# Gated cross-attention with a binarised feed-forward product on one core: rows of the large product split before they are turned, and turned by DMA

## Chip, core and metric

One core of one Trainium2 chip. The metric is the device time of one execution in microseconds (us). The engines are TensorE (PE), VectorE (DVE), ScalarE (ACT), GpSimd (POOL) and SyncE (SP), the last here only a queue that issues DMAs.

## What is computed

```python
def _L0_xattn_ref(query, key):
    a = jnp.einsum('bqd,bkd->bqk', query, key)
    e = jax.nn.softmax(a, axis=-1)
    return jnp.einsum('bqk,bkd->bqd', e, key)

def _L0_ffn_ref(x, weight_real, bias):
    W = mean(|weight_real|, per row) * sign(weight_real)
    return jnp.einsum('bsi,oi->bso', x, W) + bias

x = x + jnp.tanh(g_xattn[0]) * _L0_xattn_ref(_layernorm(x), ctx_4096)
x = x + jnp.tanh(g_ffn[0]) * _L0_ffn_ref(_layernorm(x), weight_real, bias)
```

x is (4, 1024, 2048) f32, the keys are (4, 64, 2048), the weight is 2048 x 2048.

## The kernel before

The 4096 rows of x are 32 tiles of 128 rows. A tile t goes through three stages. Stage one: its row statistics (`norm_stats1`, L678, from the row buffer `xr`), the factors of the first normalisation (`rstd1` on GpSimd, `place_factors`, and on TensorE `spread_factors`, L1067), normalisation of a second copy of the rows that lies in quadrants (`xs1`, `normalise1`, L518), the turn of rows into columns by VectorE (`turn_q`, L701), and the split into a high and a low f16 part `qt` (`high_q` on ACT, L533, `low_q` on VectorE, L721). Stage two, attention: `scores` (L1074), the maximum (`max_logits`, L732 on), `exp` (L545), `split_probs` (L742 to L748), `transpose_probs` on TensorE (L1080), `copy_pt`, and in four chunks of 512 columns `attend` (L1088) and `add_attention` (L754), each with its row statistics (`norm_stats2`); then `rstd2`, `normalise2` into `xn2` (L526), and on GpSimd `add_bias` (L455). Stage three, the large product: the normalised rows must be turned so that the 2048 columns lie on partitions. Before the change SyncE moves `xn2` into quadrants `xs2` by four DMAs (`move_x1`, L296), VectorE turns it back into `xn2` in two instructions (`turn_x1`, L701), and then `high_x1` (ACT, L541) and `low_x1` (VectorE, L726) split it into `x1t`, which has two slots. TensorE computes chunk n of y with the signs of the weights (`ffn_block`, L1096) in four blocks of 8 matmuls; VectorE scales it (`scale_y`, L765) and adds it to the rows (`add_y`, L773); SyncE stores the rows (`store`, L376).

Every engine runs a list in a fixed order, and semaphores tie the lists together. The steady part is `step(t)`: TensorE runs the 16 blocks of tile t (k = 0 to 15, n = k // 4) and, between blocks, the attention of tile t + 2 and the spread of tile t + 3. The constants in lines 75 to 79 say behind which block each piece stands: before, scores behind block 2, the transpose of the probabilities behind 4, the four `attend` behind 6 to 9, the spread behind 8. The scores wait for `q_set`, the first block of chunk n waits until the bank that it writes is free, which is `y_scaled` of two chunks before: block 8 waits for `scale_y(t, 0)`, block 0 for `scale_y(t-1, 2)` (L1165).

VectorE's order in a step (L966 to L1001) is: `finish_y(t-1, 3)`, `turn_x1(t+1)`, `max_logits` and `split_probs` of t+2, `low_x1(t+1)`, four `norm_stats1` of tile t+3, `scale_y(t, 0)`, `norm_mean1`, `add_y(t, 0)`, the four `add_attention` with their statistics and `place_factors`, `finish_y(t, 1)`, `turn_q(t+3)`, `finish_y(t, 2)`, `low_q(t+3)`. ACT's order (L651 to L664) is `high_x1(t+1)`, `exp`, `copy_pt`, `normalise1(t+3)`, `normalise2(t+2)`, `high_q(t+3)`. SyncE's order (L398 to L411) is `store(t-1)`, the reload of the same row buffer with tile t+3 once the store has landed (L380), `load_quadrants(t+3)` (L310), at one step in four the next batch's keys, and `move_x1(t+2)`. Row buffers `xr` are four, used in turn.

Ahead of the steady part lie the key preparation, the transposes of the weights by TensorE (`transpose_w`, L1043) with their signs by ACT, and the first two tiles, whose 32 blocks run as pairs between the weights' transposes, with an order written out by hand in the PAIR_ tables. Weights pass through `wstage` in 32 halves of a 128-row block; h counts them in SyncE's queue, which issues other DMAs at fixed h (L103).

Of the kernel before, what the change touches and what calls it, by code (L numbers as in the profile page):

```python
# [13 lines left out]
def flamingo_gated_kernel(  # L14
# [56 lines left out]
    w_t = weight.rearrange("(t p) (a h n) -> t h p a n", p=P, a=4, h=2)  # L71
# [3 lines left out]
    SCORES_AT, PT_AT, C_AT, SPREAD_AT = 2, 4, {6: 0, 7: 1, 8: 2, 9: 3}, 8  # L75
# [42 lines left out]
    with ExitStack() as ctx:  # L118
# [24 lines left out]
        xs2 = sb("xs2", [P, D])  # L143
# [70 lines left out]
        moved2 = sem("moved2")  # L214
# [59 lines left out]
        turned2 = sem("turned2")  # L274
        x1b_set = sem("x1b_set")
        x1_high = sem("x1_high")
        x1t_set = sem("x1t_set")
# [15 lines left out]
        def move_to_quadrants(queue, dst, src, moved):  # L293

            for a in range(4):
                queue.dma_start(dst[Q * a:Q * (a + 1), :], src[:, chunk(a)]).then_inc(moved, 16)  # L296

        def move_x1(queue, u):
            queue.wait_ge(xn2_set, u + 1)
            move_to_quadrants(queue, xs2, xn2, moved2)  # L300
# [4 lines left out]
        def _(sp):  # L305
# [16 lines left out]
            def load_w(h):  # L322
                if h >= RW:
                    before = h - RW
                    sp.wait_ge(w_tr, 2 * before + 2)
                    if before % 2 == 0:
                        sp.wait_ge(abs_dve, before // 2 + 1)
                    else:
                        sp.wait_ge(abs_act, before // 2 + 1)
                sp.dma_start(wstage[:, h % RW, :].rearrange("p (a n) -> p a n", a=4),  # L330
                             w_t[h // 2, h % 2]).then_inc(w_in[h % RW], 16)
# [20 lines left out]
            for h in range(RW, 2 * NW):  # L352
# [3 lines left out]
                if h == MOVE0_H:  # L356
                    move_x1(sp, 0)
                if h == QUADRANTS2_H:
                    load_quadrants(2)
                if h == MOVE1_H:  # L360
                    move_x1(sp, 1)
# [10 lines left out]
            move_x1(sp, 2)  # L372
# [11 lines left out]
            move_x1(sp, 3)  # L384
            store(1, 1)
            reload(1, 1, 1)
            load_quadrants(5)
            store(2, 2)
            move_x1(sp, 4)
            reload(2, 2, 1)  # L390
            load_quadrants(6)
            move_x1(sp, 5)
# [5 lines left out]
            with sp.Fori(0, LOOPS) as i:  # L398
                for j in range(STEPS):
                    t, r = i * STEPS + (FIRST + j), (FIRST + j) % RX  # L400
                    store(t - 1, (r - 1) % RX)
                    reload(t - 1, (r - 1) % RX, i + (FIRST + j - 1) // RX + 1)
# [8 lines left out]
                    move_x1(sp, t + 2)  # L411
            for t in range(FIRST + STEPS * LOOPS, NT):
                store(t - 1, (t - 1) % RX)
                if t + 3 < NT:
                    reload(t - 1, (t - 1) % RX, (t - 1) // RX + 1)
                    load_quadrants(t + 3)
                if t + 2 < NT:
                    move_x1(sp, t + 2)
# [92 lines left out]
        def _(act):  # L511
# [10 lines left out]
            def normalise2(u, r):  # L522
                act.wait_ge(nm2_set, u + 1)
                if not (isinstance(u, int) and u == 0):
                    act.wait_ge(x1t_set, u)
# [9 lines left out]
            def high_x1(u, slot):  # L535
                act.wait_ge(turned2, u + 1)
                if not isinstance(u, int) or u >= 3:
                    act.wait_ge(y_ready, u * NC - NC)
                elif u == 2:
                    act.wait_ge(y_ready, FINISHED_0)  # L540
                nc.scalar.activation(x1t[:, slot, 0, :], xn2[:, :], ACT.Copy, scale=LN_SCALE).then_inc(x1_high, 1)  # L541
# [63 lines left out]
            normalise2(0, 0)  # L605
            high_q(1)
            sign_groups(range(12, 16))
            act.wait_ge(khl_stored[0], 16)
            act.wait_ge(kd_in, 32)
            high_x1(0, 0)  # L610
# [5 lines left out]
            for k in range(PAIR_BLOCKS):  # L616
                sign_groups(pair_w[k])
                if k == NORM2_1:
                    normalise2(1, 1)
                for g in PAIR_KEYS.get(k, ()):  # L620
                    key_high(1, g)
                if k == TURN_X1_1:
                    high_x1(1, 1)
# [13 lines left out]
                if k == LOW_X1_2:  # L637
                    high_x1(2, 0)
            normalise2(3, 3)

# [3 lines left out]
            high_x1(3, 1)  # L644
# [4 lines left out]
            normalise2(4, 0)  # L649

            def step(t, r, x1=True, attention=True, ln1=True, late=False):  # L651
                if x1 and not late:
                    high_x1(t + 1, (r + 1) % 2)
# [3 lines left out]
                if late:  # L657
                    high_x1(t + 1, (r + 1) % 2)
# [7 lines left out]
            step(3, 3, late=True)  # L666
# [3 lines left out]
            for t in range(FIRST + STEPS * LOOPS, NT):  # L670
                step(t, t % RX, x1=t + 1 < NT, attention=t + 2 < NT, ln1=t + 3 < NT)

        @block.vector
        def _(dve):
# [40 lines left out]
            def turn_x1(u):  # L715
                dve.wait_ge(moved2, u * 64 + 64)
                turn(xn2, xs2).then_inc(turned2, 1)

# [5 lines left out]
            def low_x1(u, slot):  # L724
                dve.wait_ge(x1_high, u + 1)
                nc.vector.scalar_tensor_tensor(out=x1t[:, slot, 1, :], in0=xn2[:, :], scalar=LN_SCALE,  # L726
                                               in1=x1t[:, slot, 0, :], op0=ALU.mult, op1=ALU.subtract).then_inc(x1t_set, 1)
# [146 lines left out]
            turn_x1(0)  # L874
# [3 lines left out]
            low_x1(0, 0)  # L878
# [14 lines left out]
            for k in range(PAIR_BLOCKS):  # L893
# [7 lines left out]
                if k == TURN_X1_1:  # L901
                    turn_x1(1)
                for g in PAIR_KEYS.get(k, ()):
                    key_low(1, g)
                if k == LOW_X1_1:
                    low_x1(1, 1)
# [308 lines left out]
```

## Time and profile before

| | us |
|---|---|
| median of 2 runs | 1260.21 |
| the runs | 1255.38 and 1265.04 |
| span of the profiled execution, first to last instruction | 1256.9 |
| TensorE busy | 1095.5 |
| VectorE busy | 1015.0 |
| ScalarE busy | 372.4 |
| GpSimd busy | 243.1 |

The profile is one execution. Of it the span is known; the runs' median lies 3.3 us above the span, and the lower of the runs 1.5 us below it. The share of an engine is its busy time over the span. A wait row names who waited, and the instruction that ended the wait.

### The profile page before, as it was taken

The page shows a single profiled execution, that of the slowest core. Times are in us where ns is not written, and L with a number is a line of the kernel's source. Part 1 is how long each engine was busy: PE and PEld are TensorE (multiplying, and loading weights), DVE is VectorE, ACT ScalarE, POOL GpSimd, SP SyncE. Part 2 cuts the span into 40 slices and gives each one's busy share as a digit, 9 for nine tenths or more (in the row PEclk, how much of TensorE's full clock was granted, in tenths as well). Part 3 has the DMA queues.
Part 4 walks back from the last instruction along what each step waited for, and adds up shares of the span by engine and source line. Part 5 has one row for each costly group of instructions (what it writes and reads, how often), then busy time and mean ns, then how long its engine had stood idle before and what let it go on. Part 6 is the DMA issues. An engine that isn't in the chain of part 4 may idle for free.

```text
span 1256.9 us, 15376 instructions
## 1 busy us (share of the span) xinstructions
PE 1095.5 (87%) x5776; PEld 542.3 (43%) x5776; DVE 1015.0 (81%) x1258; ACT 372.4 (30%) x470; POOL 243.1 (19%) x304
## 2 busy tenths in 40 slices
PE   2478978789999999999999999999999999999998
PEld 1354643334444444444444444444444444444443
DVE  5786788887888888888888889898888888898632
ACT  3655633222223323322223322333122332333100
POOL 1121022220121222212121222221112122222100
PEclk9878998988999999999999999999999999999999
DMA  8789756254665446445675447554765546554231
GB/s 267 196 196 263 199 104 161 54 109 111 161 158 134 107 96 149 119 113 134 150 167 134 114 107 162 107 122 115 167 141 134 129 111 144 113 117 124 57 59 67
DMA packets 68782, 168.72 MB, mean 134 GB/s; under 512 B 6480, under 2 KB 24912, under 8 KB 59472
## 3 DMA queue, kind: packets, MB, share of 16 engines
q1 hardware_dynamic: 68080, 165.18, 54.7%
q0 software_dynamic: 672, 3.15, 0.8%
q8 instruction: 19, 0.31, 0.1%
q14 instruction: 11, 0.09, 0.0%
HBM read 96.47 MB, written 36.70 MB: 106 GB/s over the span
## 4 chain that ended last, share of the span: by engine, by line
PE 31%; DMA 21%; DVE 20%; ACT 9%; issue 8%; SPq 5%; POOL 4%; ACTq 0%; DVEq 0%
PE y_ps L1096 25%; DMA xs<-xn 20%; DVE xn L701 11%; ACT xn L526 5%; SPq L296 4%; PE c_ps L1088 4%; DVE xr L754 2%; DVE st L759 2%; POOL r L441 2%; ACT x1t L541 2%; POOL ve L439 1%; DMA wstage<-n_L_ffn_weight_real_dram 1%; ACT ex L545 1%; PE setup_ps L1043 1%; DVE qt L721 1%
## 5 line engine op out<-in xcount | busy, mean ns | idle before, releaser
L1096 PE MATMUL y_ps<-wsign,x1t 128*128 128x512 f16 x4096 | 948.6, 388 | 3.6 <-ACT wsign L557 2.4
L1096 PEld LDWEIGHTS y_ps<-wsign,x1t 128*128 128x128 f16 x4096 | 406.4, 100 | 492.8 <-issue 43.0
L701 DVE STREAM_TRANSPOSE xn<-xs 128x1024 f32<-128x1024 f32 x128 | 259.7, 2090 | 61.5 <-DMA xs<-xn 56.0
L439 POOL TENSOR_TENSOR ve<-mv,eps 128x1 f32<-128x1 f32 x64 | 29.2, 457 | 824.3 <-DVE mv L684 527.3
L773 DVE TENSOR_TENSOR xr<-ytmp,xr 128x512 f32<-128x512 f32 x128 | 172.6, 1348 | 3.2
L541 ACT ACTIVATE x1t<-xn 128x2048 f16<-128x2048 f32 x32 | 61.1, 1909 | 350.8 <-DVE xn L701 350.8
L455 POOL TENSOR_TENSOR xr<-xr,bias_b 128x2048 f32<-128x2048 f32 x32 | 144.9, 4527 | 72.9 <-ACT xn L526 68.1
L754 DVE SCALAR_TENSOR_TENSOR xr<-c_ps,coef,xr 128x512 f32<-128x512 f32 x128 | 95.2, 744 | 37.0 <-PE c_ps L1088 36.6
L765 DVE TENSOR_TENSOR ytmp<-y_ps,alpha_b 128x512 f32<-128x512 f32 x128 | 87.8, 686 | 43.7 <-PE y_ps L1096 39.8
L526 ACT ACTIVATE xn<-xr,nm,r 128x2048 f32<-128x2048 f32 x32 | 67.1, 2098 | 123.3 <-POOL nm L445 123.3
L518 ACT ACTIVATE xs<-xs,spread 128x512 f32<-128x512 f32 x128 | 93.8, 803 | 5.7 <-DMA xs<-in_x_dram 2.7
L759 DVE BATCH_NORM_STATS2 st<-xr 128x6 f32<-128x512 f32 x128 | 88.9, 694 | 4.4
L1088 PE MATMUL c_ps<-kd_cur,pt 128*128 128x512 f16 x256 | 79.3, 393 | 4.9 <-DVE xr L754 4.4
L1080 PE MATMUL s_ps<-ident,prob 128*128 128x128 f16 x32 | 7.8, 243 | 85.2 <-DVE prob L745 85.2
L721 DVE SCALAR_TENSOR_TENSOR qt<-xn,qt 128x2048 f16<-128x2048 f32 x32 | 76.6, 2392 | 3.3 <-ACT qt L533 3.3
L678 DVE BATCH_NORM_STATS2 st<-xr 128x6 f32<-128x512 f32 x128 | 78.8, 678 | 0.3 <-DMA xr<-in_x_dram 0.2
L726 DVE SCALAR_TENSOR_TENSOR x1t<-xn,x1t 128x2048 f16<-128x2048 f32 x32 | 73.0, 2282 | 2.0 <-ACT x1t L541 2.0
L514 ACT COPY spread<-s_ps 128x8 f32<-128x8 f32 x32 | 5.3, 166 | 232.4 <-PE s_ps L1067 232.4
L1074 PE MATMUL s_ps<-kt_cur,qt 128*128 128x128 f16 x1024 | 64.0, 222 | 9.1 <-DVE qt L721 9.0
L533 ACT ACTIVATE qt<-xn 128x2048 f16<-128x2048 f32 x32 | 61.1, 1910 | 36.4 <-DVE xn L701 36.4
L1074 PEld LDWEIGHTS s_ps<-kt_cur,qt 128*128 128x128 f16 x1024 | 61.1, 99 | 17.1 <-DVE qt L721 6.1
L1043 PE MATMUL setup_ps<-ident,wstage 128*128 128x128 f32 x256 | 42.2, 313 | 22.8 <-ACT wsign L557 12.8
(70 smaller groups left out, 402.5 us busy)
## 6 DMA issues: line engine op xcount, KB each, us to landing
xr<-in_x_dram SPq DMA_DIRECT2D x32, 1024.0 KB, 5.1
xs<-in_x_dram SPq DMA_DIRECT2D x128, 256.0 KB, 6.6
xs<-xn SPq DMA_DIRECT2D x128, 256.0 KB, 6.9
out_dram<-xr SPq DMA_DIRECT2D x31, 1024.0 KB, 3.9
wstage<-n_L_ffn_weight_real_dram SPq DMA_DIRECT2D x32, 512.0 KB, 8.3
kd_cur<-kd_dram SPq DMA_DIRECT2D x12, 512.0 KB, 5.6
kt_cur<-kt_dram SPq DMA_DIRECT2D x6, 512.0 KB, 8.0
xr<-in_ctx_dram SPq DMA_DIRECT2D x4, 512.0 KB, 6.8
```

What stands on the lines that cost most here:

```text
L455: nc.gpsimd.tensor_tensor(xr[:, r, :], xr[:, r, :], bias_b[:, :], ALU.add).then_inc(x1b_set, 1)
L518: last = nc.scalar.activation(xs1[:, chunk(c)], xs1[:, chunk(c)], ACT.Identity, bias=spread[:, 1, c:c + 1], scale=spread[:, 0, c:c + 1])
L526: nc.scalar.activation(xn2[:, :], xr[:, r, :], ACT.Identity, bias=nm2[:, :], scale=r2[:, :]).then_inc(xn2_set, 1)
L701: last = nc.vector.transpose(dst[:, D // 2 * h:D // 2 * (h + 1)].rearrange("p (k i c) -> p k c i", k=8, c=4), src[:, :].rearrange("p (c h ...
L721: nc.vector.scalar_tensor_tensor(out=qt[:, 1, :], in0=xn1[:, :], scalar=LN_SCALE, in1=qt[:, 0, :], op0=ALU.mult, op1=ALU.subtract).then_in ...
L754: nc.vector.scalar_tensor_tensor(out=xr[:, r, chunk(n)], in0=c_ps[:, n % 2, :], scalar=coef[:, 0:1], in1=xr[:, r, chunk(n)], op0=ALU.mult, ...
L759: nc.vector.bn_stats(st2[:, n, :], xr[:, r, chunk(n)]).then_inc(stats2, 1)
L765: nc.vector.tensor_tensor(ytmp[:, bank, :], y_ps[:, bank, :], alpha_b[:, chunk(n)], ALU.mult).then_inc(y_scaled, 1)
L773: nc.vector.tensor_tensor(xr[:, r, chunk(n)], ytmp[:, bank, :], xr[:, r, chunk(n)], ALU.add).then_inc(y_added, 1)
L1074: last = nc.tensor.matmul(s_ps[:, 0:P], qt[:, part, P * k:P * (k + 1)], kt_cur[:, k, :], start=(k == 0 and part == 0), stop=(k == ND - 1 a ...
L1088: last = nc.tensor.matmul(c_ps[:, n % 2, :], pt[:, :], kd_cur[:, part, chunk(n)], start=(part == 0), stop=(part == 1))
L1096: last = nc.tensor.matmul(y_ps[:, bank, :], x1t[:, slot, part, P * k:P * (k + 1)], wsign[:, k, chunk(n)], start=(k == 0 and part == 0), st ...
```

## The change

`xn2` is no longer moved, turned and then split; it is split as it lies (rows on partitions) into a new f16 buffer `x1n`, high part by ACT directly behind `normalise2`, low part by VectorE, and both parts are turned by two transposing DMAs of SyncE into `x1t`. The contraction index thereby lies in its natural order, and the weights are loaded and transposed in natural order too. TensorE waits for the DMAs (`x1_turned`, 32 per tile) where it waited for `x1t_set`. ACT's order in a step becomes `exp`, `copy_pt`, `normalise1`, `high_q`, `normalise2`, `high_x1(t+2)`. In VectorE's order `turn_x1` goes and `low_x1(t+1)` takes its place. On TensorE the transpose of the probabilities moves from behind block 4 to behind 6, `attend` from 6 to 9 to 7 to 10, the spread from 8 to 11. SyncE's loop is written out instead of looped by register. The buffer `xs2` goes.

```diff
-    w_t = weight.rearrange("(t p) (a h n) -> t h p a n", p=P, a=4, h=2)
-    SCORES_AT, PT_AT, C_AT, SPREAD_AT = 2, 4, {6: 0, 7: 1, 8: 2, 9: 3}, 8
+    w_t = weight.rearrange("(t p) (h n) -> t h p n", p=P, h=2)
+    SCORES_AT, PT_AT, C_AT, SPREAD_AT = 2, 6, {7: 0, 8: 1, 9: 2, 10: 3}, 11
...
-    NORM2_1, TURN_X1_1, LOW_X1_1 = 1, 3, 4
-    NORM2_2, TURN_X1_2, LOW_X1_2 = 23, 27, 29
-    BIAS_H, MOVE0_H, QUADRANTS2_H, MOVE1_H, X2_H, X3_H, QUADRANTS3_H = 5, 7, 10, 15, 20, 21, 27
+    NORM2_1, LOW_X1_1 = 1, 3
+    NORM2_2, LOW_X1_2 = 23, 27
+    BIAS_H, TURN0_H, QUADRANTS2_H, TURN1_H, X2_H, X3_H, QUADRANTS3_H = 5, 9, 10, 19, 20, 21, 27
...
+        def wait_x1(queue, u):
+            queue.wait_ge(x1_low, u + 1)
+            if not isinstance(u, int) or u >= 3:
+                queue.wait_ge(y_ready, u * NC - NC)
+            elif u == 2:
+                queue.wait_ge(y_ready, FINISHED_0)
+        def turn_x1(queue, slot):
+            for part in range(2):
+                queue.dma_start_transpose(x1t[:, slot, part, :].rearrange("p (k i) -> p k i", i=P),
+                                          x1n[:, part, :]).then_inc(x1_turned, 16)
...
-            with sp.Fori(0, LOOPS) as i:
+            for i in range(LOOPS):
                 for j in range(STEPS):
                     t, r = i * STEPS + (FIRST + j), (FIRST + j) % RX
+                    wait_x1(sp, t + 1)
                     store(t - 1, (r - 1) % RX)
+                    turn_x1(sp, (r + 1) % 2)
                     reload(t - 1, (r - 1) % RX, i + (FIRST + j - 1) // RX + 1)
                     load_quadrants(t + 3)
...
-                    move_x1(sp, t + 2)
...
-            def high_x1(u, slot):
-                act.wait_ge(turned2, u + 1)
+            def high_x1(u):
+                if not (isinstance(u, int) and u == 0):
+                    act.wait_ge(x1_turned, u * 32)
+                act.wait_ge(xn2_set, u + 1)
+                nc.scalar.activation(x1n[:, 0, :], xn2[:, :], ACT.Copy, scale=LN_SCALE).then_inc(x1_high, 1)
...
             def step(t, r, attention=True, ln1=True):
                 if attention:
                     exp(t + 2)
                     copy_pt(t + 2)
                 if ln1:
                     normalise1(t + 3)
+                    high_q(t + 3)
                 if attention:
                     normalise2(t + 2, (r + 2) % RX)
-                if ln1:
-                    high_q(t + 3)
+                    high_x1(t + 2)
...
                 finish_y(t - 1, 3, (r - 1) % RX)
                 if x1:
-                    turn_x1(t + 1)
+                    low_x1(t + 1)
                 if attention:
                     max_logits(a)
                     split_probs(a)
-                if x1:
-                    low_x1(t + 1, (r + 1) % 2)
...
-                rows = wstage[:, h % RW, :].rearrange("p (m k) -> p k m", k=8)
-                through_bank(("w", m), lambda b: rows[:, GROUP * (m % 2) + b], w_tr)
+                through_bank(("w", m), lambda b: wstage[:, h % RW, P * (GROUP * (m % 2) + b):P * (GROUP * (m % 2) + b + 1)], w_tr)
...
-                pe.wait_ge(x1t_set, t + 1)
+                pe.wait_ge(x1_turned, t * 32 + 32)
```

For t = 28 to 30 SyncE keeps `store(t-1)` first, then waits and turns. At the start it waits for x1 of tiles 0 and 1 between weight loads (h = 9 and 19), and for the copies of the keys from the same space before the first.

## Rows read from the trace of the kernel before

**Rows 1.** The page, part 1: busy time of each engine.
```profile
PE 1095.5 (87%) x5776; PEld 542.3 (43%) x5776; DVE 1015.0 (81%) x1258; ACT 372.4 (30%) x470; POOL 243.1 (19%) x304
```
**Rows 2.** The waits: who for whom, us in total, times, longest.
```profile
PE s_ps L1080 <- DVE prob L745: 85.2, 31, 3.8
```
**Rows 3.** TensorE's timeline, the transpose of the probabilities (start, length, [idle before]).
```profile
294.04 0.29 PE L1080 MATMUL s_ps<-ident,prob 128*128 128x128 f16 x1 [3.04 <-DVE prob L745]
...
1174.91 0.23 PE L1080 MATMUL s_ps<-ident,prob 128*128 128x128 f16 x1 [2.71 <-DVE prob L745]
```
**Rows 4.** The timeline of all engines, 599 to 670: from spread to split.
```profile
631.65 4.06 DVE L701 STREAM_TRANSPOSE xn<-xs 128x1024 f32<-128x1024 f32 x2
...
632.98 2.10 ACT L526 ACTIVATE xn<-xr,nm,r 128x2048 f32<-128x2048 f32 x1 [3.67 <-POOL nm L445]
...
635.15 4.54 POOL L455 TENSOR_TENSOR xr<-xr,bias_b 128x2048 f32<-128x2048 f32 x1 [2.21 <-ACT xn L526]
...
635.75 1.91 ACT L533 ACTIVATE qt<-xn 128x2048 f16<-128x2048 f32 x1 [0.67 <-DVE xn L701]
636.27 3.97 DVE L773 TENSOR_TENSOR xr<-ytmp,xr 128x512 f32<-128x512 f32 x1
640.16 2.28 DVE L721 SCALAR_TENSOR_TENSOR qt<-xn,qt 128x2048 f16<-128x2048 f32 x1
...
660.07 0.35 PE L1067 MATMUL s_ps<-factors,same_i 128*128 128x8 f32 x2
...
660.74 2.93 ACT L518 ACTIVATE xs<-xs,spread 128x512 f32<-128x512 f32 x4
```
**Rows 5.** The same timeline: one step on TensorE and VectorE.
```profile
644.05 1.95 PE L1074 MATMUL s_ps<-kt_cur,qt 128*128 128x128 f16 x32
...
652.23 0.23 PE L1080 MATMUL s_ps<-ident,prob 128*128 128x128 f16 x1 [2.78 <-DVE prob L745]
...
652.30 3.62 PE L1096 MATMUL y_ps<-wsign,x1t 128*128 128x512 f16 x16
...
654.42 2.46 DVE L678 BATCH_NORM_STATS2 st<-xr 128x6 f32<-128x512 f32 x4
...
655.75 0.59 PE L1088 MATMUL c_ps<-kd_cur,pt 128*128 128x512 f16 x2
...
656.18 1.89 PE L1096 MATMUL y_ps<-wsign,x1t 128*128 128x512 f16 x8
656.91 0.69 DVE L765 TENSOR_TENSOR ytmp<-y_ps,alpha_b 128x512 f32<-128x512 f32 x1
```
**Rows 6.** A slow stretch: timeline, and the windows view (PE, PEld, DVE, ACT, POOL, PEclk, DMA, GB/s).
```profile
616.33 5.30 PE L1096 MATMUL y_ps<-wsign,x1t 128*128 128x512 f16 x16
...
616.00:620.00 4.00, 3.74 (x12) 1.46 (x13) 4.00 (x7) 0.27 (x1) 0.00 (x0) 0.66 0.98 230
```
**Rows 7.** The page, part 5: groups of instructions (busy, mean ns | idle before).
```profile
L678 DVE BATCH_NORM_STATS2 st<-xr 128x6 f32<-128x512 f32 x128 | 78.8, 678 | 0.3 <-DMA xr<-in_x_dram 0.2
L726 DVE SCALAR_TENSOR_TENSOR x1t<-xn,x1t 128x2048 f16<-128x2048 f32 x32 | 73.0, 2282 | 2.0 <-ACT x1t L541 2.0
```
**Rows 8.** The timeline, SyncE's queue in the same step: store and reload.
```profile
643.93 0.37 SPq L376 DMA_DIRECT2D out_dram<-xr  x1
...
647.98 0.34 SPq L380 DMA_DIRECT2D xr<-in_x_dram  x1
```
**Rows 9.** The DMA view: issues, KB each, median us to landing.
```profile
xr<-in_x_dram SPq DMA_DIRECT2D x32, 1024.0 KB, 5.1
...
xs<-xn SPq DMA_DIRECT2D x128, 256.0 KB, 6.9
out_dram<-xr SPq DMA_DIRECT2D x31, 1024.0 KB, 3.9
...
kt_cur<-xn SPq DMA_DIRECT2D x1, 512.0 KB, 3.7
```

More of the change, by code:

```diff
@@ L213, in flamingo_gated_kernel @@
         xs1_in = sem("xs1_in")
-        moved2 = sem("moved2")
+        x1_turned = sem("x1_turned")
         ones_set = sem("ones_set")
@@ L355, in _ @@
                     sp.dma_start(bias_b[:, :], bias.partition_broadcast(P)).then_inc(bias_in, 16)
-                if h == MOVE0_H:
-                    move_x1(sp, 0)
+                if h == TURN0_H:
+                    sp.wait_ge(khl_stored[0], 16)
+                    sp.wait_ge(kd_in, 32)
+                    wait_x1(sp, 0)
+                    turn_x1(sp, 0)
                 if h == QUADRANTS2_H:
                     load_quadrants(2)
-                if h == MOVE1_H:
-                    move_x1(sp, 1)
+                if h == TURN1_H:
+                    wait_x1(sp, 1)
+                    turn_x1(sp, 1)
                 if h == X2_H:
@@ L383, in _ @@
             reload(0, 0, 1)
-            move_x1(sp, 3)
+            wait_x1(sp, 2)
+            turn_x1(sp, 0)
             store(1, 1)
@@ L387, in _ @@
             load_quadrants(5)
+            wait_x1(sp, 3)
+            turn_x1(sp, 1)
             store(2, 2)
-            move_x1(sp, 4)
             reload(2, 2, 1)
             load_quadrants(6)
-            move_x1(sp, 5)
+            wait_x1(sp, 4)
+            turn_x1(sp, 0)
             sp.wait_ge(kts_stored[0], 16)
@@ L410, in _ @@
                         load_kd(batch)
-                    move_x1(sp, t + 2)
             for t in range(FIRST + STEPS * LOOPS, NT):
                 store(t - 1, (t - 1) % RX)
+                if t + 1 < NT:
+                    wait_x1(sp, t + 1)
+                    turn_x1(sp, (t + 1) % 2)
                 if t + 3 < NT:
@@ L649, in _, with step @@
             normalise2(4, 0)
-            def step(t, r, x1=True, attention=True, ln1=True, late=False):
-                if x1 and not late:
-                    high_x1(t + 1, (r + 1) % 2)
+            high_x1(4)
+            def step(t, r, attention=True, ln1=True):
                 if attention:
@@ L656, in step @@
                     copy_pt(t + 2)
-                if late:
-                    high_x1(t + 1, (r + 1) % 2)
                 if ln1:
                     normalise1(t + 3)
+                    high_q(t + 3)
                 if attention:
                     normalise2(t + 2, (r + 2) % RX)
-                if ln1:
-                    high_q(t + 3)
-            step(3, 3, late=True)
+                    high_x1(t + 2)
+            step(3, 3)
             with act.Fori(0, LOOPS) as i:
@@ L670, in _ @@
             for t in range(FIRST + STEPS * LOOPS, NT):
-                step(t, t % RX, x1=t + 1 < NT, attention=t + 2 < NT, ln1=t + 3 < NT)
+                step(t, t % RX, attention=t + 2 < NT, ln1=t + 3 < NT)
         @block.vector
@@ L722, in low_q, with low_x1 @@
                                                op0=ALU.mult, op1=ALU.subtract).then_inc(q_set, 1)
-            def low_x1(u, slot):
+            def low_x1(u):
                 dve.wait_ge(x1_high, u + 1)
-                nc.vector.scalar_tensor_tensor(out=x1t[:, slot, 1, :], in0=xn2[:, :], scalar=LN_SCALE,
-                                               in1=x1t[:, slot, 0, :], op0=ALU.mult, op1=ALU.subtract).then_inc(x1t_set, 1)
+                nc.vector.scalar_tensor_tensor(out=x1n[:, 1, :], in0=xn2[:, :], scalar=LN_SCALE,
+                                               in1=x1n[:, 0, :], op0=ALU.mult, op1=ALU.subtract).then_inc(x1_low, 1)
             def max_logits(u):
@@ L873, in _ @@
             sum_abs(3)
-            turn_x1(0)
+            low_x1(0)
             max_logits(1)
@@ L947, in _ @@
             turn_q(4)
-            turn_x1(3)
+            low_x1(3)
             low_q(4)
             finish_y(2, 1, 2)
-            low_x1(3, 1)
             max_logits(4)
@@ L1007, in _ @@
             finish_y(3, 0, 3)
-            turn_x1(4)
+            low_x1(4)
             add_attention(5, 1, 0)
@@ L1016, in _ @@
             norm_stats2(5, 1, 2)
-            low_x1(4, 0)
             add_attention(5, 1, 3)
@@ L1136, in _ @@
                     if n == 0:
-                        pe.wait_ge(x1t_set, tile + 1)
+                        pe.wait_ge(x1_turned, 32 * tile + 32)
                     if k >= 8:
```

50 lines of the change are left out of this document (11 added, 39 removed).

## The prediction

> **What bounds the kernel now.** I read the page's first part, then the waits, then TensorE's timeline over all steps, and last one step of all engines in order of time. TensorE is busy 87% of the span [rows 1], and its largest wait is for the probabilities: 85.2 us in 31 waits [rows 2]. The transpose of the probabilities (L1080) comes once per step, at 294.04 and for the 26th time at 1174.91 us, so 25 steps of the steady part take 880.87 us, 35.2 us each [rows 3]. In one step 16 matmuls of the large product last 3.45 us (652.30 to 655.75), so a block of 8 is 1.73; a pair for the attention output 0.43 (655.75 to 656.18), the scores 1.8 to 1.95 [rows 5]. Sixteen blocks (27.7), four such pairs (1.7), the scores, the spread and the transpose make 31.5 us. The rest is the wait of 2.8 us [rows 3, 5] and, in about half the steps, a slower stretch after it: at 616.33 sixteen matmuls take 5.30 us where others take 3.62, and the granted clock of 616 to 620 is 0.66, a mix of the two levels (1.2 and 2.4 GHz), right after TensorE had idled 2.8 us [rows 5, 6]. That costs 1.7. So TensorE sets the pace, held up once a step by VectorE. What is not a bound yet, but close: VectorE's row statistics of the next tile (L678) start at 654.42 [rows 5]; their tile's load was issued at 647.98 [rows 8] and takes 5.1 us [rows 9], so it landed at 653.1, only 1.3 us early. The groups show almost no wait there (0.3 us in all, [rows 7]).
>
> **What goes.** Per tile two VectorE transposes (4.03 us together, like the ones at 631.65, [rows 4]) and four moves by DMA. The wait for the probabilities has less in front of it: between y's last chunk and the scores' maximum there is only low_x1 (2.28, [rows 7]) instead of the wait for the moves and the transpose; and the transpose of the probabilities is due two blocks (3.45 us) later. Both alone would take the 2.8 us away, and with it the slow stretch.
>
> **What is added.** Two transposing DMAs of 512 KB per tile. And an order: in the loop SyncE first waits for x1_low(t+1), then stores tile t-1, then issues the two transposes, then waits for the store, then reloads the row buffer. Behind that wait stand the store, the reload and the loads of the quadrants; for the reload wait VectorE's four statistics, which stand in its queue before scale_y(t, 0), and for that waits TensorE's block 8 (n = 2 needs the bank of n = 0). The spread of the factors is now behind block 11. These close a loop that did not bind before. I follow it from the start S of the spread:
> - ACT copies and normalises the quadrants, done 3.6 after S (660.07 to 660.74 + 2.93, [rows 4]).
> - turn_q 4.06 on VectorE: 7.7. high_q on ACT 1.91: 9.6. low_q 2.28: 11.9 [rows 4]. Between them finish_y(t, 2) fits.
> - ACT now does normalise2 behind high_q, 2.10: 11.7; GpSimd's add_bias starts 0.07 later and takes 4.54 [rows 4], to 16.3.
> - scale_y(t, 3) 0.69 [rows 5]: 12.6. add_y(t, 3) falls on add_bias. The row at 636.27 shows what that does: the sum took 3.97 us instead of 0.64 to 0.69 and ended 0.55 after GpSimd's at 639.69 [rows 4]. Before it was chunk 2 that met it, now chunk 3: it ends at 16.8.
> - low_x1 2.28: 19.1. The store is issued at 19.2. The reload follows 4.05 later (643.93 to 647.98, [rows 8]) at 23.25, and lands 5.1 later [rows 9]: 28.3.
> - Statistics 2.46, scale_y 0.69 [rows 5]: 31.5. TensorE's blocks 8 to 11 with the three pairs between them, 4 x 1.73 + 3 x 0.43 = 8.2: the next spread at 39.7.
> So the loop takes 39.7 us even if the transposes disturbed nothing, against 35.2 now. TensorE, whose own work ends after 31.5, stands at block 8 for 7 us and more; the rows after its idle time [rows 6] say that the clock is then at the lower level for a while: 1.7 us, on this path. 41.4.
>
> **The transposes' price, X.** No row shows a transposing DMA. They are issued straight behind the store, and the reload is queued behind them. Let D be the time in which the two pass. The store lands after 3.9, the transposes by 3.9 + D, the reload some 4.2 later (its 5.1 less what overlaps; the store of the same size takes 3.9): 8.1 + D after the store, where the chain above has 9.15. So X = D - 1, and not below nothing. From below: D = 0, hidden in the store's round trip, X = 0, 41.4 a step; as fast as the store, D = 3.9, X = 3. From above by the nearest row: the four moves of the same megabyte, 2.6 us to issue and 6.9 to land behind the last of them [rows 9], D some 10, X = 9; that it is more than that, no row excludes. The row nearest in shape is the copy within SBUF of 512 KB over all partitions, 3.7 us each [rows 9]: two in turn, with some overlap, D = 6. I take X = 5, so 46.4 us a step.
> The Trainium skill ("Advanced Engine Details and Errata", X-Bar Transpose (TRN2)) holds that transposing DMAs are as fast as regular ones, 350 to 400 GB/s: D would be an estimated 2.8, and the total some 1457. The Trainium skill ("VectorE: DVE Perf Modes", The three transpose paths) gives 1309 ns for a single 128x128 block; if the 32 blocks of a tile passed one by one that would be an estimated 42 us. No row here decides between them; the sum uses neither.
>
> **The rest.** Weights come in longer runs and are read by TensorE unstrided: 0, at best the few us that it waited for them. At the start low_x1(0) is free of VectorE's transpose, but SyncE's queue of weight loads now stands behind wait_x1(0) and wait_x1(1), with transposes between: I take gain against loss, 0, with 15 us either way. Step 29 (no reload any more) loses its wait, -3. The last two steps are TensorE's alone. Unrolling SyncE's loop: nothing, that queue idles most of each step.
>
> **Sum.** Steps 4 to 28 have reload and statistics: 25 x (46.4 - 35.2) = +280; -3; on the span of 1256.9 that is 1534. The median of the runs shown lies 3.3 above the span: 1537.
>
> **Rivals.**
> - *Transposes at a plain copy's speed.* Same loop, X = 3: 44.4 a step, 25 x 9.2 = +230, about 1487. For it: all data stay in SBUF and use all partitions; against it: the moves within SBUF were the slowest megabyte in the table. The rule of the Trainium skill told above belongs here. Chance 0.22. Where they hide entirely (X = 0) it is 1257 + 155 = 1412; without the clock's 1.7, 1370. Chance of this corner 0.08.
> - *Transposes far slower than any row.* D = 15: X = 14, 55.4 a step, +505, about 1762. Then SyncE's later loads are late as well; from D = 35 on TensorE also waits for x1 at the start of a step. Chance 0.15.
> - *The other side: the reload is in time.* Then the loop falls to TensorE's own 31.5 plus the 1.2 by which scale_y(t, 2), now behind turn_q (8.4 after S), keeps block 0 of the next step (due 7.2 after S) waiting: 32.7, 25 x -2.5 = -62, about 1195. It decides at one point: block 8 is due 24.6 after S, so the statistics must start by 21.4, and the row load must have landed 2.2 us after the store was issued. Store and load take 9.2 in turn. It holds only if the store were issued at 12 after S, which the stretched sum, low_x1 and the new order all forbid. Chance 0.05.
> - *Half of it:* the stretched sum vanishes (-4.1 us) with fast transposes: 37 to 38 a step less the clock's share, within some per cent of now. Chance 0.04.
> My forecast has 0.46.
>
> **The numbers.** 1537. Range 1410 to 1760: it leaves out the corner of hidden transposes and below, and the far end of slow ones. A measurement here tells about 2% from no change: faster 0.05, within 0.03, slower 0.92.
>
> **What would show it.** Right: VectorE's L678 waits for the load of x, 6 us and more in 25 steps, and TensorE waits for ytmp (L765) at y's third chunk; the wait for the probabilities is gone; the transpose of the probabilities comes every 44 to 50 us; SyncE's wait before the store is for low_x1, and its reload for the store; one sum of L773 per step is still 4 us; the granted clock falls in each step. Wrong: no wait at L678, or a step under 40 us; or TensorE waiting for x1_turned at a step's start, which would mean D beyond 35.

## The result, and the profile after

| | before | after |
|---|---|---|
| median of 2 runs, us | 1260.21 | 1518.12 |
| the runs, us | 1255.38, 1265.04 | 1515.89, 1520.35 |
| span of the profiled execution, us | 1256.9 | 1514.1 |
| ratio after / before | | 1.202, 95% interval 1.187 to 1.217 |

The changed kernel is 20% slower; 1537 was forecast, with 1410 to 1760 as the range. One kernel below, e4, had a granted clock of 0.56 from start to end in its profiled execution; that execution is not compared, and the kernel was run again as e5.

The page after, part 1 and TensorE's granted clock, against [rows 1]:

```profile
PE 1127.7 (74%) x5776; PEld 548.9 (36%) x5776; DVE 900.7 (59%) x1194; ACT 372.7 (25%) x470; POOL 247.4 (16%) x304
PEclk9789999898888998888988889988889888889999
```

VectorE lost 114 us of work (its 64 transposes for x1, which are gone, were 131; the sums of `add_y` grew by 8), and nobody gained by it: TensorE's share fell from 87 to 74%. The waits view names the new ones, against [rows 2]:

```profile
PE y_ps L1083 <- DVE ytmp L762: 295.5, 77, 11.7
DVE st L679 <- DMA xr<-in_x_dram: 282.7, 26, 11.9
PE y_ps L1083 <- DMA x1t<-x1n: 15.8, 3, 7.9
```

The wait for the probabilities, 85.2 us in [rows 2], is no longer among the long ones. In its place TensorE waits 295 us for a scaled chunk of y (L762 is `scale_y`), and VectorE waits 283 us, 11 us in each step, for the row load, where [rows 7] had 0.3 in all. TensorE's timeline, the transpose of the probabilities, against [rows 3]:

```profile
337.26 0.22 PE L1067 MATMUL s_ps<-ident,prob 128*128 128x128 f16 x1
...
1393.93 0.22 PE L1067 MATMUL s_ps<-ident,prob 128*128 128x128 f16 x1
```

Between these two lie 23 steps: 1056.67 / 23 = 45.94 us a step, against 35.2. No wait stands in front of them now. The chain of waits of one step shows the loop closed (start us, us, what):

```profile
744.57 2.21 DVE x1n L723
...
746.80 0.34 SPq L381
747.15 0.04 issue
747.19 4.85 SPq L302
752.04 0.04 issue
752.08 2.00 SPq L302
...
754.12 6.19 DMA xr<-in_x_dram
...
760.34 0.07 DVE st L679
...
762.84 0.70 DVE ytmp L762
763.54 0.04 issue
763.59 3.59 PE y_ps L1083 x8
...
774.69 0.14 PE s_ps L1054 x2
774.82 0.02 issue
774.84 0.17 ACT spread L524
```

low_x1 (L723), then the store (L381), then 6.85 us in which SyncE is held in the two transposing DMAs (L302), then the row load, the statistics, scale_y, block 8 and the way to the spread. Block 8 takes 3.59 us instead of 1.73: TensorE had stood for 11.3 us, and the windows view has its granted clock at the lower of its two levels (1.2 GHz, the 0.50 of the first row) right behind that wait and back at 1.00 eight us later (PE, PEld, DVE, ACT, POOL, PEclk, DMA share, GB/s):

```profile
763.00:767.00 4.00, 3.41 (x9) 1.21 (x10) 2.88 (x7) 0.00 (x0) 1.46 (x4) 0.50 0.18 35
...
771.00:775.00 4.00, 3.81 (x20) 1.85 (x17) 3.22 (x5) 0.16 (x1) 0.00 (x0) 1.00 0.00 0
```

### The profile page after: what moved, and what is told of

The parts are those of the page before. It is cut to its first block, busy times and chain, and to the rows that moved or that the text cites. A ratio compares the mean times of both kernels' runs of the same rounds, so it can differ in the third digit from the quotient of the medians.

```text
span 1514.1 us, 14944 instructions
## 1 busy us (share of the span) xinstructions
PE 1127.7 (74%) x5776; PEld 548.9 (36%) x5776; DVE 900.7 (59%) x1194; ACT 372.7 (25%) x470; POOL 247.4 (16%) x304
## 2 busy tenths in 40 slices
DMA packets 171183, 168.73 MB, mean 111 GB/s; under 512 B 137552, under 2 KB 139600, under 8 KB 161872
## 3 DMA queue, kind: packets, MB, share of 16 engines
q1 hardware_dynamic: 170480, 165.18, 40.7%
## 4 chain that ended last, share of the span: by engine, by line
PE 28%; DVE 24%; SPq 13%; DMA 13%; issue 12%; ACT 9%; POOL 1%; DVEq 0%; ACTq 0%; POOLq 0%
PE y_ps L1083 23%; SPq L302 11%; DMA xr<-in_x_dram 10%; DVE xr L770 6%; DVE xn L702 5%; ACT xs L528 4%; DVE st L679 4%; DVE x1n L723 4%; ACT qt L543 4%; PE c_ps L1075 3%; DVE ytmp L762 3%; DMA x1t<-x1n 1%; PE setup_ps L1031 1%; DMA wstage<-n_L_ffn_weight_real_dram 1%; DVE qt L718 1%
## 5 line engine op out<-in xcount | busy, mean ns | idle before, releaser
L1083 PE MATMUL y_ps<-wsign,x1t 128*128 128x512 f16 x4096 | 976.9, 395 | 313.2 <-DVE ytmp L762 295.5
L465 POOL TENSOR_TENSOR xr<-xr,bias_b 128x2048 f32<-128x2048 f32 x32 | 148.0, 4624 | 254.0 <-ACT xn L536 249.2
L770 DVE TENSOR_TENSOR xr<-ytmp,xr 128x512 f32<-128x512 f32 x128 | 180.5, 1410 | 3.2
L702 DVE STREAM_TRANSPOSE xn<-xs 128x1024 f32<-128x1024 f32 x64 | 128.7, 2065 | 58.3 <-ACT xs L528 58.3
L762 DVE TENSOR_TENSOR ytmp<-y_ps,alpha_b 128x512 f32<-128x512 f32 x128 | 86.9, 679 | 59.8 <-PE y_ps L1083 55.9
L1075 PE MATMUL c_ps<-kd_cur,pt 128*128 128x512 f16 x256 | 83.0, 409 | 0.4 <-ACT pt L560 0.4
L723 DVE SCALAR_TENSOR_TENSOR x1n<-xn,x1n 128x2048 f16<-128x2048 f32 x32 | 72.9, 2278 | 0.0
L549 ACT ACTIVATE x1n<-xn 128x2048 f16<-128x2048 f32 x32 | 61.2, 1911 | 5.1 <-DMA x1t<-x1n 2.3
L553 ACT ACTIVATE ex<-logits,neg_max,lscale 128x64 f32<-128x64 f32 x32 | 14.0, 439 | 180.9 <-DVE neg_max L734 180.9
```

Source lines behind the costliest of these rows:

```text
L465: nc.gpsimd.tensor_tensor(xr[:, r, :], xr[:, r, :], bias_b[:, :], ALU.add).then_inc(x1b_set, 1)
L702: last = nc.vector.transpose(dst[:, D // 2 * h:D // 2 * (h + 1)].rearrange("p (k i c) -> p k c i", k=8, c=4), src[:, :].rearrange("p (c h ...
L723: nc.vector.scalar_tensor_tensor(out=x1n[:, 1, :], in0=xn2[:, :], scalar=LN_SCALE, in1=x1n[:, 0, :], op0=ALU.mult, op1=ALU.subtract).then_ ...
L762: nc.vector.tensor_tensor(ytmp[:, bank, :], y_ps[:, bank, :], alpha_b[:, chunk(n)], ALU.mult).then_inc(y_scaled, 1)
L770: nc.vector.tensor_tensor(xr[:, r, chunk(n)], ytmp[:, bank, :], xr[:, r, chunk(n)], ALU.add).then_inc(y_added, 1)
L1075: last = nc.tensor.matmul(c_ps[:, n % 2, :], pt[:, :], kd_cur[:, part, chunk(n)], start=(part == 0), stop=(part == 1))
```

## The experiments

The question was no longer whether the loop exists but what each of its members is worth, whether the transposing DMAs themselves are the loss or only their place, and whether the change's second part, the later transpose of the probabilities, is innocent. Step lengths are taken as above, over 23 steps from the second transpose of the probabilities in the steady part to the last but one.

### e1: the load ahead of the transposes

Against the changed kernel, as all diffs below are unless another is named:

```diff
                     wait_x1(sp, t + 1)
                     store(t - 1, (r - 1) % RX)
-                    turn_x1(sp, (r + 1) % 2)
                     reload(t - 1, (r - 1) % RX, i + (FIRST + j - 1) // RX + 1)
                     load_quadrants(t + 3)
+                    turn_x1(sp, (r + 1) % 2)
```

> In the loop SyncE keeps its wait for low_x1 first and the store second, but issues the reload and the quadrants' loads ahead of the two transposes. Theory (a step of 45.9 us is one loop: spread, turn, add, low_x1, store, transposes' issue, reload, statistics, scale_y, four blocks, spread): the reload follows the store after 4.1 us instead of 7.1 to 7.3 and lands 5.1 to 5.3 later instead of 5.9 to 6.2, so a step is 41.8 and the span 1514 - 24 x 4.1 = 1416. Rival 1 (the wait at the statistics is a symptom, something else paces the step): no change, 1500 to 1520. Rival 2 (the transposes of the step before clog the queue whatever their place): the reload keeps its 6.2 and only part is won, 1440.

Measured: 1404.9 us, span 1405.5, ratio to before 1.110 (1.097 to 1.123), a step of 41.25. Its timeline, SyncE's queue:

```profile
706.83 0.34 SPq L381 DMA_DIRECT2D out_dram<-xr  x1
...
710.71 0.34 SPq L385 DMA_DIRECT2D xr<-in_x_dram  x1
711.10 2.58 SPq L313 DMA_DIRECT2D xs<-in_x_dram  x4
...
713.72 10.08 SPq L302 DMA_TRANSPOSE x1t<-x1n  x2
```

The load follows the store after 3.9 us again, and its median landing is back at 5.0. So the transposes' place in the queue costs 4.7 us a step. Rival 1 and rival 2 fall. SyncE is held for 10.1 us in the transposes now (9.2 to 10.3 in the steps), with 2 MB of loads ahead of them; in the steps nothing waits for that.

### e2: the store freed of low_x1 as well

Against e1's kernel:

```diff
-                    wait_x1(sp, t + 1)
                     store(t - 1, (r - 1) % RX)
                     reload(t - 1, (r - 1) % RX, i + (FIRST + j - 1) // RX + 1)
                     load_quadrants(t + 3)
+                    wait_x1(sp, t + 1)
                     turn_x1(sp, (r + 1) % 2)
```

> In the loop SyncE issues store, reload and quadrants first, and only then waits for low_x1 and issues the transposes. Theory: beyond e1 the store no longer waits for low_x1 (2.28 us), a step is 39.5 and the span 1514 - 24 x 6.4 = 1360, still slower than before (1257), because even an undisturbed store and reload of 9.2 us now stand in a loop with VectorE's stretched sum and four blocks of TensorE. Rival (the new order in SyncE's queue is the whole loss): the time falls to that of before or under it, 1200 to 1257.

Measured: 1363.7 us, span 1362.4, ratio 1.077 (1.065 to 1.089), a step of 39.39. The rival, that SyncE's order is the whole loss, falls: with the old order of store and load restored the kernel is still 8% slower than before. The rest of the loop is the store and the load in turn, which still take 8.9 us from the store's issue to the landed rows, and what VectorE and TensorE do between them.

### e3: the statistics out of scale_y's way, SyncE as changed

```diff
-                if ln1:
-                    for n in range(NC):
-                        norm_stats1(a1, ra1, n)
-                    stats1_done(a1)
-                scale_y(t, 0, r)
-                if ln1:
-                    norm_mean1(a1)
-                add_y(t, 0, r)
+                finish_y(t, 0, r)
                 for n in range(NC):
                     if attention:
                         add_attention(a, ra, n)
                         norm_stats2(a, ra, n)
-                    if ln1 and n == 0:
-                        place_factors(a1)
+                    if ln1 and n == 2:
+                        for m in range(NC):
+                            norm_stats1(a1, ra1, m)
+                        stats1_done(a1)
+                    if ln1 and n == 3:
+                        norm_mean1(a1)
...
                 add_y(t, 1, r)
+                if ln1:
+                    place_factors(a1)
```

> SyncE as changed; on VectorE the four statistics of the next tile go behind scale_y(t, 0), add_y(t, 0) and three of the attention's adds, and place_factors behind add_y(t, 1). Theory: TensorE's block 8 no longer waits for the row load; the load lands 32.5 us after the spread, statistics, mean, the rest of VectorE's queue and GpSimd's chain bring the next spread to 39, so the span is 1514 - 24 x 6.9 = 1350; TensorE's wait for ytmp of 295 us falls under 60, and a wait for the factors or for ytmp's second chunk takes a part of it. Rival (VectorE's order does not matter, since the load is late anyway): a step stays at 45 and more.

Measured: 1348.4 us, span 1347.2, ratio 1.065 (1.053 to 1.078), a step of 39.05. The wait for the scaled chunk is gone (1.3 us are left of the 295), and TensorE now waits for the factors, as expected:

```profile
PE s_ps L1053 <- DVE factors L710: 133.7, 29, 7.5
```

So one member of the loop is VectorE's order: an instruction that waits for a late DMA stands in front of one that TensorE needs. Taking it out is worth as much as all of SyncE's order in e2, though the load lands as late as ever.

### e4 and e5: the block positions of before in the changed kernel

```diff
-    SCORES_AT, PT_AT, C_AT, SPREAD_AT = 2, 6, {7: 0, 8: 1, 9: 2, 10: 3}, 11
+    SCORES_AT, PT_AT, C_AT, SPREAD_AT = 2, 4, {6: 0, 7: 1, 8: 2, 9: 3}, 8
```

> The changed kernel with the block positions of before (transpose of the probabilities behind block 4, attend 6 to 9, spread 8); everything else as changed. Theory: between block 8's start, which waits for scale_y, and the spread lies one block instead of four and three pairs, 6.5 us less in the loop: a step of 39.4, a span of 1514 - 24 x 6.5 = 1358, and no wait for the probabilities comes back above 0.5 us, since they are due later than they are ready. Rival (moving the blocks was a gain, hidden under the loss from the DMAs): undoing it costs the 2.8 us of wait again, 1514 or up to 1580.

Its other execution took 1402.7 us where 1358 was expected: the direction held, the size did not. So the same kernel again:

> The kernel of e4 once more, for a trace at the ordinary clock (e4's profiled execution had a granted clock of 0.56 throughout). One undisturbed time of e4 was 1402.7, a step of 41.3 where 39.4 was expected. Theory: block 8 itself runs in the slow stretch behind the wait (3.4 us instead of 1.73), so that only 4.7 of the 6.5 us are won; to be seen as 0.43 us matmuls between scale_y and the spread, and no wait for the probabilities. Rival: the factors are late and TensorE waits for them at the spread for 1 to 2 us. Second rival: a wait for the probabilities of 1 to 2 us is back.

Measured: 1405.0 us, span 1408.2, ratio 1.109 (1.094 to 1.124), a step of 41.46, 4.5 less than the changed kernel's. The timeline of TensorE and VectorE from scale_y to the spread:

```profile
723.67 0.69 DVE L762 TENSOR_TENSOR ytmp<-y_ps,alpha_b 128x512 f32<-128x512 f32 x1
...
724.41 3.51 PE L1083 MATMUL y_ps<-wsign,x1t 128*128 128x512 f16 x8 [8.29 <-DVE ytmp L762]
...
726.51 0.22 DVE L710 TENSOR_SCALAR factors<-own_c,nm 128x4 f32<-128x4 f32 x1
...
727.76 0.28 PE L1054 MATMUL s_ps<-factors,same_i 128*128 128x8 f32 x2
...
728.37 2.93 ACT L528 ACTIVATE xs<-xs,spread 128x512 f32<-128x512 f32 x4
...
733.54 4.01 DVE L702 STREAM_TRANSPOSE xn<-xs 128x1024 f32<-128x1024 f32 x2
```

Block 8 takes 3.4 us from its start to the spread; the factors had been ready for a microsecond. Both rivals of e5 fall. The signs that e5's theory named are there, and its 4.7 us are near the 4.5 measured, but its reason does not hold: in the changed kernel block 8 is as slow, so that cannot be what is missing. Between block 8's start and the spread even more is won than the 6.5 us expected: a mean of 10.3 us before and 3.3 now, over the steps from 380 to 1080 us. What is lost lies behind the spread. ACT has the quadrants normalised at 731.30, but `turn_q` starts only at 733.54, since VectorE still has the last adds of the attention and `finish_y(t, 1)` in its list. That is 5.8 us after the spread instead of 3.6, and takes 2.3 of the 7.0 us back.

### e6: the block positions alone, in the kernel before

```diff
-    SCORES_AT, PT_AT, C_AT, SPREAD_AT = 2, 4, {6: 0, 7: 1, 8: 2, 9: 3}, 8
+    SCORES_AT, PT_AT, C_AT, SPREAD_AT = 2, 6, {7: 0, 8: 1, 9: 2, 10: 3}, 11
```

> The kernel before with the new block positions alone (transpose of the probabilities behind block 6, attend 7 to 10, spread 11); the moves and VectorE's turn stay. Theory (the loop from the spread): turn_q ends 7.7 after the spread, add_y(2) stretched 10.9, low_q 13.1, the third chunk's add 14.5, the moves land 15.9, turn to 19.9, probabilities 23, low_x1 25.3, statistics 27.7, scale_y 28.4, blocks 8 to 11 with three pairs 8.2: a step of 36.7 to 38.4 instead of 35.2, span 1290 to 1337: the second part of the change is a loss by itself. Rival (the plain reading of the waits: 2.8 us per step go away): 1160 to 1190.

Measured: 1335.8 us, span 1334.7, ratio 1.054 (1.043 to 1.066), a step of 38.37. TensorE's timeline:

```profile
716.57 0.23 PE L1080 MATMUL s_ps<-ident,prob 128*128 128x128 f16 x1 [0.35 <-DVE prob L745]
...
722.00 3.43 PE L1096 MATMUL y_ps<-wsign,x1t 128*128 128x512 f16 x8 [3.04 <-DVE ytmp L765]
```

The wait for the probabilities fell from 2.8 to 0.35 us as it was meant to, and 3.0 us of waiting for scale_y came two blocks later, with the slow stretch behind it, now in all steps but the first. No DMA is different in this kernel. The second part of the change is by itself a loss of 5%: the spread, moved behind block 11, lengthens a loop that had been shorter than the step. It is not the loop through the row load, which lands 1.4 us before VectorE comes to the statistics, but VectorE's own list from `turn_q` to `scale_y`.

### e7: one transposing DMA instead of two

```diff
-            for part in range(2):
-                queue.dma_start_transpose(x1t[:, slot, part, :].rearrange("p (k i) -> p k i", i=P),
-                                          x1n[:, part, :]).then_inc(x1_turned, 16)
+            queue.dma_start_transpose(x1t[:, slot, :, :].rearrange("p a (k i) -> p (a k) i", i=P),
+                                      x1n[:, :, :].rearrange("p a n -> p (a n)")).then_inc(x1_turned, 16)
```

with the waits for `x1_turned` at 16 per tile.

> The changed kernel with one transposing DMA of 1 MB per tile instead of two of 512 KB. Theory: the 6.6 us for which SyncE is held in the two instructions are back-pressure of the data in its queue, not a cost per instruction: one instruction takes some 6.5, a step stays at 45.9, 1505 to 1525. Rival (3.3 us for each instruction whatever its size): 3.3 less per step, 1435.

Measured: 1520.0 us, span 1518.8, a step of 45.98. SyncE's queue:

```profile
703.62 7.22 SPq L301 DMA_TRANSPOSE x1t<-x1n  x1
710.89 0.58 SPq L384 DMA_DIRECT2D xr<-in_x_dram  x1
```

One instruction holds the queue for 7.2 us, the two had for 6.2 to 7.1. The rival, a price per instruction, falls. That it is the data ahead that hold the instruction fits e1, where it was held 10.1 us behind 2 MB of loads, and the last tiles of the changed kernel, where with only a store issued 2.2 us ahead the two take 4.6 to 5.1; what in the issuing engine makes it wait was not tried.

### e8: the loop opened at both ends

e2's order in SyncE's queue, and on VectorE:

```diff
-                if ln1:
-                    for n in range(NC):
-                        norm_stats1(a1, ra1, n)
-                    stats1_done(a1)
-                scale_y(t, 0, r)
-                if ln1:
-                    norm_mean1(a1)
-                add_y(t, 0, r)
+                finish_y(t, 0, r)
                 for n in range(NC):
...
                     if ln1 and n == 0:
-                        place_factors(a1)
+                        for m in range(NC):
+                            norm_stats1(a1, ra1, m)
+                        stats1_done(a1)
+                    if ln1 and n == 1:
+                        norm_mean1(a1)
+                    if ln1 and n == 2:
+                        place_factors(a1)
```

> The changed kernel with e2's order in SyncE's queue (store, reload and quadrants ahead of the wait for low_x1 and the transposes), and on VectorE the statistics behind the attention's first add, their mean behind the second, the factors behind the third. Theory: the load lands 25.8 us after the spread, where VectorE now reaches the statistics at 26.5; nothing waits for them, the spread is due at 32.7 and its factors are ready at 32, so a step is TensorE's 31.5 plus 1.2 for scale_y(t, 2) behind turn_q: 32.7, 1514 - 24 x 13.2 = 1197, faster than before by 4 to 5%. Rival (transposes themselves cost the core time in some other way, by slowing every other DMA or SBUF access): 1257 or more.

Measured: 1201.7 us, span 1199.4, ratio 0.948 (0.938 to 0.959), a step of 32.86. The changed kernel, with the same DMAs and the same block positions, is 5% faster than before once two queues are reordered. The rival, a cost of the transposes in themselves, falls. One wait is left in TensorE's step, at block 12:

```profile
701.54 12.26 PE L1082 MATMUL y_ps<-wsign,x1t 128*128 128x512 f16 x56 [1.42 <-DVE ytmp L762]
```

The theory had put its 1.2 us at block 0, for `scale_y(t, 2)` behind `turn_q`. There is no wait there (block 0 runs within the 56 matmuls of this row); the 1.42 us are at block 12, for `scale_y(t, 1)`. That the two figures are close, and the step of 32.86 so near 32.7, is luck.

### e9: chunks 1 and 2 of y earlier

Against e8's kernel:

```diff
                 for n in range(NC):
+                    if n == 3:
+                        scale_y(t, 1, r)
                     if attention:
                         add_attention(a, ra, n)
...
-                scale_y(t, 1, r)
+                add_y(t, 1, r)
                 if attention:
                     norm_mean2(a)
-                add_y(t, 1, r)
+                finish_y(t, 2, r)
                 if ln1:
                     turn_q(a1)
-                finish_y(t, 2, r)
-                if ln1:
                     low_q(a1)
```

> e8's kernel with two more steps of VectorE moved: scale_y(t, 1) ahead of the attention's last add, and finish_y(t, 2) ahead of turn_q. In e8's step of 32.9 us TensorE waits 1.4 us for ytmp at the fourth chunk. Theory: that wait goes, and the one at the next step's first chunk, which would come in its place (scale_y(t, 2) behind turn_q), does not arise; what is left is TensorE's own 31.5, with perhaps 0.8 where the row load, 25.8 us after the spread, holds the statistics and so the factors: 31.5 to 32.3 a step, 1199 - 24 x (0.6 to 1.4) = 1166 to 1185. Rival (the step is by now bound elsewhere, by the DMAs or the clock): 1195 to 1205.

Measured: 1188.4 us, span 1185.5, ratio 0.939 (0.935 to 0.942), a step of 32.38, just over the range. The rival falls. The 1.4 us went, and a part of the 0.9 us that are left above 31.5 is the load, as supposed: VectorE waits for it, and the factors come 0.2 to 0.4 us late:

```profile
720.92 2.47 DVE L679 BATCH_NORM_STATS2 st<-xr 128x6 f32<-128x512 f32 x4 [0.76 <-DMA xr<-in_x_dram]
...
727.05 0.39 PE L1053 MATMUL s_ps<-factors,same_i 128*128 128x8 f32 x2 [0.20 <-DVE factors L710]
```

### e10: ACT's order as well

Against e9's kernel:

```diff
                 if ln1:
                     normalise1(t + 3)
-                    high_q(t + 3)
                 if attention:
                     normalise2(t + 2, (r + 2) % RX)
                     high_x1(t + 2)
+                if ln1:
+                    high_q(t + 3)
```

> e9 with ACT's normalise2 and high_x1 ahead of high_q in the steady steps, as normalise2 was before the change. Theory: GpSimd's add_bias then runs 5.7 to 10.3 us after the spread, under turn_q, and no longer stretches the third chunk's add (4.3 us instead of 0.69), so the store leaves 2.3 to 3 us earlier, the load lands at 23 and the factors are in time: 31.5 a step, 1166 to 1172, at or below e9. Rival (add_bias stretches low_q instead, by as much, and the scores wait for it): 1185 to 1200, slower than e9.

Measured: 1178.1 us, span 1179.2, ratio 0.930 (0.927 to 0.934), a step of 32.03; faster than e9 by 10 us, and 6 us over the range given. Its timeline:

```profile
699.41 4.54 POOL L465 TENSOR_TENSOR xr<-xr,bias_b 128x2048 f32<-128x2048 f32 x1 [2.21 <-ACT xn L536]
...
703.17 2.93 DVE L719 SCALAR_TENSOR_TENSOR qt<-xn,qt 128x2048 f16<-128x2048 f32 x1 [2.23 <-ACT qt L543]
...
706.16 1.96 PE L1061 MATMUL s_ps<-kt_cur,qt 128*128 128x128 f16 x32 [0.49 <-DVE qt L719]
706.74 0.69 DVE L771 TENSOR_TENSOR xr<-ytmp,xr 128x512 f32<-128x512 f32 x1
```

GpSimd's add_bias no longer meets the last chunk's add (0.69 us against 4.30), but it does meet low_q, which takes 2.93 us instead of 2.28, and the scores wait 0.5 us for it. So the rival's mechanism is there, with 0.65 us of stretch where the add had 3.6.

### e11: the same orders without the DMAs

The kernel before, with the block positions of the change and VectorE's order of e9; moves and VectorE's turn as before.

> The kernel before (moves by DMA, VectorE's turn) with the new block positions and VectorE's order of e9: statistics behind the attention's first add, scale_y(t, 1) ahead of the last, finish_y(t, 2) ahead of turn_q. Theory (the transposing DMAs are worth having once the loop through the row load is open): with VectorE's turn left in, the moves land 15.8 us after the spread, the turn ends at 19.8, the probabilities are ready at 23 where they are due at 21.1, the statistics, mean and factors follow late, some 34.2 a step and a slow stretch in some steps: 1225 to 1250, 4 to 6% over e10. Rival (the gain of e9 and e10 is all from the order, none from the DMAs): 1175 to 1190.

Measured: 1247.3 us, span 1244.4, ratio to before 0.988 (0.983 to 0.993), a step of 34.74. The rival falls: e10 is 7.0% faster than before, and the block positions and VectorE's order alone give 1.2%. The wait for the probabilities stays in part (1.5 us a step), since the moves and the turn still stand before it:

```profile
DVE xn L701 <- DMA xs<-xn: 70.4, 30, 5.0
...
PE s_ps L1079 <- DVE prob L745: 45.8, 29, 2.9
```

## Why the prediction was right

- *The loop.* Followed from the spread at 727.79 in the trace after: turn_q starts at 731.36, 3.57 later (3.6 forecast), low_q ends at 739.6 (11.8; 11.9), add_y of chunk 3 takes 4.30 us and ends at 744.6 (16.8; 16.8), the store leaves at 746.80 (19.0; 19.2). Four members are shown by an edit each: the transposes' place (e1, 4.7 us), low_x1 ahead of the store (e2, 1.9), the statistics ahead of scale_y (e3, 6.9), the blocks before the spread (e5, 4.5). The stretched add was taken out only in e10, when this loop hardly set the pace any more; the others are read from the trace.
- *X, the transposes' price.* 5 was taken; store to landed load is 746.80 to 760.34, 13.5 us, against 9.15, so X = 4.4, and 3.8 in the step before (701.54 to 714.53); over the steps from 380 to 1080 us the median is 4.0. The size was right within about a microsecond, but that was in part luck, since the working was not the one given. I had the reload issued once the store had landed, and then wait behind the transposes in the DMA queue. The trace has SyncE itself held in the two instructions for 6.85 us, so that the reload is issued 7.3 us after the store instead of 4.05; that is 3.3 of X, and only 1.1 is the slower landing (6.2 for 5.1). One sign that the prediction named is therefore not there: the reload does not wait for the store, which lands 4.4 us after its issue (median), but for SyncE to be free. e7 shows that one instruction of the whole size holds it as long. The prediction also called the moves within SBUF the slowest megabyte in the table; keys and weights take longer to land for half as much (8.0 and 8.3 us for 512 KB), so that this argument against fast transposes was weak.
- *The rule of the Trainium skill* ("Advanced Engine Details and Errata", X-Bar Transpose (TRN2)), transposes as fast as regular DMAs at 350 to 400 GB/s, would have given an estimated X = 1.8. The trace does not bear it out for these transfers: for the last tiles, where only a store left 2.2 us ahead of them, the two instructions hold the queue for 4.6 to 5.1 us, each lands 4.6 to 4.9 us after its issue, and both together 6.9 us after the first's issue, where a plain store of the same megabyte takes 3.9 and a load 5.1 [rows 9]. The 1309 ns for a 128x128 block ("VectorE: DVE Perf Modes", The three transpose paths) is no rate either: each of these transfers turns 16 such blocks, and all have landed within 4.8 us (median of the 64).
- *The clock.* 1.7 us a step were put on the path. From block 8's start to the spread the steps from 380 to 1080 us have 9.5 to 11.1 us, with a median of 10.1: 1.3 to 2.9 above the 8.2 at full speed, which e8 shows as 8.20.
- *Sum.* 46.4 a step was forecast, 45.94 measured. The difference of the traces is 257 us, where 277 was the sum. The 25 steps counted are the right ones (the 26 transposes of the probabilities from 293.7 to 1436.2 us, in the trace before from 294.0 to 1174.9), and they differ by 262 us instead of 280: 23 of them are the 45.94, the first (43.6) and the last (42.25) are shorter. Behind them the changed kernel is 4 us shorter, where 3 had been put.
- *The start*, put at nothing with 15 us either way, cost nothing: TensorE waits three times, 15.8 us in all, for the transposing DMAs, but its first block of tile 4, with which the steady part begins, starts at 279.8 us where it started at 280.4 before. What makes the waits up was not taken apart.
- *The other side.* The rival with the reload in time was priced at 32.7 us a step and 1195. It could not hold for this change, where the load lands 32 us after the spread and had to by 21.4. e8 measured 32.86 and 1202, but by another way: its load lands at 25.8, and it is the statistics that stand later in VectorE's list.
- *Where it fell short* was the change's second part. The prediction said that the later transpose of the probabilities would take the 2.8 us away, "with it the slow stretch", and counted the spread's new place only within the loop. e6 shows it as a loss of 72 us on its own (1335.8 against 1263.7 for the kernel before, measured beside it), with a slow stretch in all steps but the first.

## What to carry over

A wait row tells what ends a wait, not what its removal gives: in an order of fixed lists, find the loop that will be the longest once the wait is gone, add it up, and compare it with the bound engine's own work. When an instruction is moved later to give its input time, ask who waits for what is behind it; and put what waits for a late transfer behind what another engine needs. In a queue of DMAs the transfer with a deadline goes first, and the one with a whole step of time, here the transposes, goes last.

## What was not expected of the hardware

- A transposing DMA holds its issuing queue: a median of 2.77 us for 512 KB (about 4.8 for the first of a pair in the steps and 1.9 for the second, up to 5.5), 7.2 for 1 MB, against 0.35 us for a plain store of 1 MB. Its data go in packets of 256 B: the page after counts 137,552 packets under 512 B, before 6,480, and the 131,072 more are 2048 for each of the 64 DMAs.
- Even so they load the DMA engines less than the moves they replace: in the 23 steps the windows view has a DMA share of 0.56 of 809 us before and 0.39 of 1057 after, some 453 and 412 us, at the same data per step. Over the whole span the queue's packets took 54.7% before (688 us) and 40.7% after (616 us), at the same 165 MB; the part of that which lies ahead of the steps (some 30 us) can be the weights' loads as well, whose order had changed too.
- The slow stretches are gone with the long waits: the granted clock is 1.00 in e9 and e10 over windows of 100 us in the middle of the run (300 to 400, 500 to 600, 800 to 900), where before it was 0.97 in each of the three. It is 1.00 in e8 and e11 too, where TensorE still waits 1.4 and 1.5 us once a step. With the waits of 2.6 to 3.0 us of the kernel before it fell in 14 of 26 cases; in e6, with 3.0 us and more, in all steps but the first (2.8 us), and in the changed kernel, with 8 to 12 us, in all 25.
